# Order of work in the first and last channel pair of a chunk, in a fused state-space and FFN layer on one core

## What is computed

```python
# layer 1: state-space layer (DIN = 2048 channels, N = 16 states, R = 64, K = 4 taps)
h = layernorm(x)
xs, z = split(h @ in_proj_w)                 # 2048 channels each
xc = silu(conv_b + sum_k conv_w[:, k] * shifted(xs, k))
p = xc @ x_proj_w.T                          # 64 + 16 + 16 columns
dt_r, B, C = rmsnorm(p[:, :64]), rmsnorm(p[:, 64:80]), rmsnorm(p[:, 80:])
dt = softplus(dt_r @ dt_proj_w.T + dt_bias)
# per channel d and state n, over time t:
s[t, d, n] = exp(dt[t, d] * A[d, n]) * s[t-1, d, n] + dt[t, d] * B[t, n] * xc[t, d]
y[t, d] = sum_n s[t, d, n] * C[t, n]
x = x + ((y + D * xc) * silu(z)) @ out_proj_w.T
# layer 2: quantised FFN
x = x + layernorm(x) @ (scales * (codes - 128)).T + bias
```

## Time and profile before

| | |
|---|---|
| median of three runs | 4553.35 us |
| profiled execution | 4553.78 us, its span 4552.0 us |
| mean granted TensorE clock | 0.976 |
| TensorE (PE) busy | 4257.0 us, 94% |
| VectorE (DVE) busy | 4156.6 us, 91% |
| GpSimd (POOL) busy | 3887.0 us, 85% |
| ScalarE (ACT) busy | 3534.8 us, 78% |
| DMA | 828.91 MB, mean 182 GB/s |

### The profile page before, as it was taken

One profiled execution on the slowest core, in us unless ns is written; L12 is line 12 of the kernel. 1 busy time (PEld: TensorE's weight loads), 2 busy tenths in 40 slices (PEclk: granted clock), 3 DMA queues, 4 the chain that ended last, 5 costly groups with the idle time before them and its releaser, 6 DMA issues.

```text
span 4552.0 us, 77871 instructions
## 1 busy us (share of the span) xinstructions
PE 4257.0 (94%) x25632; PEld 3830.9 (84%) x25632; DVE 4156.6 (91%) x5745; ACT 3534.8 (78%) x8848; POOL 3887.0 (85%) x2894
## 2 busy tenths in 40 slices
PE   7688989999999999999999999999999999998879
PEld 6567778888888888888888888988888898897769
DVE  3899999999999999999999999999999999999871
ACT  3788787888888788787888888787888878888750
POOL 0898989989898998989899898998989899899870
PEclk9788999999999999999999999999999999998889
DMA  7545556575756657575575757557575665755452
GB/s 247 160 122 184 150 183 184 164 224 174 220 166 196 192 174 220 163 227 163 176 218 165 234 155 219 175 156 242 155 226 168 209 189 147 226 167 178 133 150 85
DMA packets 201348, 828.91 MB, mean 182 GB/s; under 512 B 25456, under 2 KB 34416, under 8 KB 151792
## 3 DMA queue, kind: packets, MB, share of 16 engines
q1 hardware_dynamic: 141296, 639.35, 38.6%
q0 software_dynamic: 41216, 151.01, 18.7%
q10 hardware_dynamic: 18432, 33.56, 2.0%
HBM read 634.57 MB, written 55.05 MB: 151 GB/s over the span
## 4 chain that ended last, share of the span: by engine, by line
PE 60%; POOL 19%; DVE 10%; issue 7%; ACT 2%; DMA 1%; SPq 0%; POOLq 0%; DVEq 0%; ACTq 0%
PE ys L646 14%; POOL dbx L494 12%; PE gx L626 12%; PE ys L606 12%; PE g L799 10%; PE g L721 7%; DVE hb L1416 6%; POOL half L518 3%; POOL half L512 3%; DVE gx L1298 1%; PE ys L636 1%; PE hb L901 1%; DVE hc L1364 1%; DMA ybuf<-in_wf_scales 1%; POOL hd L507 1%
## 5 line engine op out<-in xcount | busy, mean ns | idle before, releaser
L494 POOL TENSOR_TENSOR dbx<-dtx,bb 128x1024 f32<-128x1024 f32 x1024 | 2427.4, 2370 | 231.1 <-DVE hb L1416 183.8
L1416 DVE TENSOR_TENSOR_SCAN hb<-hb,dbx 128x512 f32<-128x512 f32 x2048 | 2495.6, 1219 | 55.4 <-ACT hb L1111 27.3
L1111 ACT ACTIVATE hb<-dt,a_neg 128x256 f32<-128x256 f32 x4096 | 1789.1, 468 | 66.3
L606 PE MATMUL ys<-half,ident 128*128 128x256 f32 x3072 | 811.6, 400 | 162.6 <-POOL half L512 93.6
L799 PEld LDWEIGHTS g<-wo,ybuf 128*128 128x128 f32 x7680 | 919.2, 194 | 30.7 <-issue 14.7
L646 PE MATMUL ys<-xnT,wz 128*128 128x256 f32 x4096 | 926.2, 385 | 11.4 <-DVE ybuf L1375 11.4
L799 PE MATMUL g<-wo,ybuf 128*128 128x128 f32 x7680 | 928.3, 277 | 8.4 <-issue 8.4
L626 PE MATMUL gx<-xnT,wx 128*128 128x256 f32 x3968 | 895.4, 383 | 21.5 <-issue 10.9
L646 PEld LDWEIGHTS ys<-xnT,wz 128*128 128x128 f32 x4096 | 782.6, 193 | 127.8 <-DVE ybuf L1375 22.8
L626 PEld LDWEIGHTS gx<-xnT,wx 128*128 128x128 f32 x3968 | 750.6, 192 | 127.3 <-issue 14.3
L606 PEld LDWEIGHTS ys<-half,ident 128*128 128x128 f32 x3072 | 567.4, 195 | 302.2 <-POOL half L512 125.0
(11 more groups left out here) (108 smaller groups left out, 3145.5 us busy)
## 6 DMA issues: line engine op xcount, KB each, us to landing
wz<-in_win SPq DMA_DIRECT2D x128, 1024.0 KB, 5.0
hd<-hd POOLq DMA_DIRECT2D x256, 512.0 KB, 6.3
wx<-in_win SPq DMA_DIRECT2D x124, 1024.0 KB, 5.0
wo<-in_wout SPq DMA_DIRECT2D x123, 1024.0 KB, 7.3
wf<-wf_scratch SPq DMA_DIRECT2D x113, 512.0 KB, 3.6
xc_scratch<-xcn ACTq DMA_DIRECT2D x128, 256.0 KB, 2.7
xcs<-xc_scratch SPq DMA_DIRECT2D x128, 256.0 KB, 5.2
bb<-bc_scratch SPq DMA_DIRECT2D x64, 512.0 KB, 9.6
```

The costliest lines, as they stand in the source:

```text
L494: nc.gpsimd.tensor_tensor(dbx[:, k % 2, :].rearrange("p (n t) -> p n t", n=NQ), dtx[:, S % 2, a, :].unsqueeze(1).to_broadcast([P, NQ, T]), ...
L606: mm = nc.tensor.matmul(ys[i // 3][:, 0:T], ident[:], half[:, n % PLACES, w * T:(w + 1) * T], start=False, stop=(i % 3 == 2 and w == 1), s ...
L1111: ins = nc.scalar.activation(h[:, m * T:(m + 1) * T], dt[:, j % 2, a, :], ACT.Exp, scale=a_neg[:, ds((2 * j + a) * N + 2 * v + m, 1)])
L1416: nc.vector.tensor_tensor_scan(h[:], h[:], dbx[:, k % 2, w * UW:(w + 1) * UW], 0.0, ALU.mult, ALU.add).then_inc(scans, 1)
```

## The change

In the last pair: TensorE's list gives x, dt and the three sums of tile 0 ahead of the last output part, which now stands directly ahead of z; the output part before is cut in two. ScalarE's x_taps and VectorE's taps move up, ahead of the softplus and of scan 13. In the first and last pair: VectorE's gate of tile 0 moves from behind product 11 to behind product 12, and the output add with the norm's statistics from behind product 12 to behind product 13. On SyncE the four loads of B's rows go ahead of the pair's weights, those of C in between and behind, and wx is loaded behind wo, dtw and C's third group. Ordinary pairs keep their order; `out_proj` only takes its bounds in another form.

```diff
@@ -384,11 +384,15 @@
                         sp.wait_ge(l2_tr, after(4 * (c - 1)))
                         sp.dma_start(xrow[:], x_rows[c + 2]).then_inc(xrow_in, 16)
                     if last and st.inproj:
+
                         bc_rows(c + 1)
-                        for q in range(2):
-                            load_b(c + 1, q)
-                            load_c(c + 1, q)
-                    if nx.x_job(nx_last):
+                        load_b(c + 1, 0)
+                        load_b(c + 1, 1)
+                        load_c(c + 1, 0)
+                        load_b(c + 1, 2)
+                        load_c(c + 1, 1)
+                        load_b(c + 1, 3)
+                    if not last and nx.x_job(nx_last):
                         load_pair(S + PAIRS + 2)
                     if nx.outproj:
                         sp.wait_ge(o_mm, after(S - PAIRS + 1))
@@ -397,9 +401,11 @@
                         sp.wait_ge(dt_mm, after(S + 2))
                         sp.dma_start(dtw[:], dtw_in[j_x]).then_inc(dtw_in_s, 16)
                     if last and st.inproj:
-                        for q in range(2, NQ):
-                            load_b(c + 1, q)
-                            load_c(c + 1, q)
+                        load_c(c + 1, 2)
+                    if last and nx.x_job(nx_last):
+                        load_pair(S + PAIRS + 2)
+                    if last and st.inproj:
+                        load_c(c + 1, 3)
                     if nx.next_scan(nx_last):
                         sp.wait_ge(z_mm, after(S + 2))
                         sp.dma_start(wz[:].rearrange("p a b -> p (a b)"), win[j_x + PAIRS]).then_inc(wz_in, 16)
@@ -781,10 +787,11 @@
                             pe.wait_ge(y_ready, after(2 * S + 1))
                         pair_z(S + 1, a)
 
-                    def out_proj(part):
+                    def out_proj(lo, hi):
+
                         if not st.outproj:
                             return
-                        if part == 0:
+                        if lo == 0:
                             pe.wait_ge(wo_in, landed(PAIRS // 2 + S - PAIRS + 1))
                             if first:
                                 pe.wait_ge(y_ready, after(2 * c * PAIRS))
@@ -792,7 +799,7 @@
                                 g1_after_f()
                             else:
                                 g1_after_o()
-                        for kt in range(part * TILES // 4, (part + 1) * TILES // 4):
+                        for kt in range(lo, hi):
                             for tt in range(TT):
 
 
@@ -801,7 +808,7 @@
                                                            (kt % 2) * T + tt * P:(kt % 2) * T + (tt + 1) * P],
                                                       wo[:, kt, :], start=(kt == 0 and tt == 0),
                                                       stop=(kt == TILES - 1), skip_group_check=True)
-                        if part == 3:
+                        if hi == TILES:
                             mm.then_inc(o_mm, 1)
 
                     def dt_proj():
@@ -822,27 +829,28 @@
                     if last and st.norm1:
                         norm1(0)
                         x_proj()
-                        out_proj(0)
+                        out_proj(0, 4)
                         norm1(1)
-                        out_proj(1)
+                        out_proj(4, 8)
                         norm1(2)
-                        out_proj(2)
+                        out_proj(8, 10)
                         norm1(3)
+                        out_proj(10, 12)
                         x_in_proj(0)
                         ss_transpose()
-                        out_proj(3)
+                        x_in_proj(1)
                         dt_proj()
-                        x_in_proj(1)
                         group(0)
                         group(1)
                         group(2)
+                        out_proj(12, 16)
                     elif first and st.ffn:
-                        out_proj(0)
-                        out_proj(1)
+                        out_proj(0, 4)
+                        out_proj(4, 8)
                         x_proj()
-                        out_proj(2)
+                        out_proj(8, 12)
                         norm2(0)
-                        out_proj(3)
+                        out_proj(12, 16)
                         norm2(1)
                         group(0)
                         dt_proj()
@@ -1232,14 +1240,14 @@
                     unit(11)
                     norm2(3)
                     unit(12)
-                    if not edge:
+                    if not edge or last:
                         x_taps()
                     dt_softplus()
                     unit(13)
                     first_decays_out()
                     second_skip_term()
                     unit(14)
-                    if edge:
+                    if edge and not last:
                         x_taps()
                     unit(15)
 
@@ -1509,16 +1517,23 @@
                     product(10)
                     scan(12)
                     product(11)
-                    y_gate(S, 0)
                     if not edge:
+                        y_gate(S, 0)
+                    if not edge or last:
                         taps()
                     scan(13)
                     product(12)
-                    add_out()
-                    norm_stats()
+                    if edge:
+                        y_gate(S, 0)
+                    else:
+                        add_out()
+                        norm_stats()
                     scan(14)
                     product(13)
                     if edge:
+                        add_out()
+                        norm_stats()
+                    if edge and not last:
                         taps()
                     scan(15)
                     product(14)
```

## The result

The changed kernel takes 4559.77 us (median of 22 runs, 4556.12 to 4564.15) against 4553.46 of the kernel before on the same chip (22 runs, 4549.43 to 4558.11): +6.3 us, a ratio of 1.0014 with a 95% interval of 1.0007 to 1.0020: slower, clear of noise, but by less than 0.2%. The busy times hardly moved (the page, part 1; before: the earlier trace rows); what moved is where engines wait.

What follows compares the result with a forecast made beforehand. VectorE and TensorE are both over 90% busy, no single bound; the loss sits at chunk edges. -11.4 - 2.7 + 0.5 + 3.7 + 21.6 + 0.7 = +12.4 us: 4566, own range 4556 to 4578, full range 4541 to 4585.

Steps and rivals of the forecast that it cites:

- its signs: Edges: z over 8 us at most, VectorE waiting 3 to 4 us at L1332, first pairs near 39 us.
- TensorE's and ScalarE's part: Last pair: sums done 2.5 us earlier, but taps ahead of the softplus; scan 13 waits 0.55 us.
- z late, at a steady clock zero: Edge: z starts at 2266.1 instead of 2264.01; VectorE's 1.95 us lead is all given back at L1332.
- B's rows: First pair: earlier B loads end GpSimd's dbx wait, 0.8 us per edge, bounds 0.5 and 0.84.
- First pair: Gate and output add move; the 1.62 us wait only shifts to scan 13; 0.15 us left, bounds 0 and 0.3.
- Chunk 15: Its first pair has no x projection to cover z, so gate and z come later: +3.7 us.
- Edges 0 to 1 and 1 to 2: Early edges: -2.7 us at 1 to 2, without FFN ahead; +0.5 and clock +0.7 at 0 to 1.
- The clock: TensorE's clock falls after 3.3 us idle ahead of z: 1.8 us per edge, 12 x 1.8 = +21.6, bounds 0.6 and 3.4.
- DMA: SyncE's reordered loads at the edge: as many bytes, each needed 10 us or more after its issue.
- Rival 1: The clock holds over TensorE's idle time, losing under 0.8 us per edge; B rows win: -9.9, 4543; chance 0.21.
- rival 3: Gate no longer waits, z's delay not felt, VectorE keeps 1.95 us per edge: 35 less, 4520; chance 0.04.
- Rival 2: Clock stays down through all of z: 3.4 us per edge instead of 1.8, +19 more, 4585; chance 0.13.

Runs made afterwards that it cites:

- The filler: Changed kernel plus six dummy matmuls between the last output part and z in each last pair; 4542.22 us, ratio 0.9982 to the kernel before.
- the early gate: Changed kernel with the last pair's gate of tile 0 back behind product 11, ahead of the filter; 4550.38 us, ratio 0.9999 to the kernel before.
- the best version: Changed kernel with last and first pairs' gate and first pair's output add at old places, xrow loaded in second pair; 4515.68 us, 0.9919 of the kernel before.

## Why the prediction was right, and where it was off

The direction and the path were as forecast: z late, an idle TensorE ahead of it, a fall of the clock, a wait at the output add. The size was half, 4559.8 against 4566, inside the forecast's own range. At +0.14% it also lies within the 0.2% of no change to which the prediction gave a chance of 0.16. Of its signs, z was over 8 us at 8 of 12 edges, the add waited 3.8 us at six and about 5 at two, and first pairs took 38.4 us on average (forecast near 39).

- **TensorE's and ScalarE's part** held to about a tenth: last pair 35.1 (forecast 35.2), wait at scan 13 0.47 (0.55), z 2.0 us later (2.1) behind 3.28 us idle (3.3), no wait at the gate.
- **z late, at a steady clock zero**: the add waited 2.11 us where the clock held (2.0), and such an edge is 72.21 us against the average of 73.13 before, -0.92 (forecast -0.95). The filler shows it at all twelve.
- **B's rows**: 0.72 us per edge by themselves (0.8 taken, bounds 0.5 to 0.84). What the prediction did not see is that late z would have covered most of their wait: in this kernel the new loads bring some 4 us, not 10. At full clock an edge takes 73.13 us with the old order and old loads (the average), 72.41 with the new loads alone, 72.4 with the new order alone and 72.21 with both. So either gain hides most of the other: the first to be made wins about 0.7 us, the second then 0.2. The sum, 0.8 for the loads and 0.15 for the rest, is not touched by it, since the edge with both came out as forecast.
- **First pair**: the wait only moved from the gate to scan 13, as said. Chunk 15: +4.1 us in the second pair, where +3.7 was forecast, and +0.5 in the first, which the sum had left out: scan 13 waits 2.47 us there instead of 1.83, behind the softplus.
- **Edges 0 to 1 and 1 to 2**: -2.1 up to chunk 2's last pair, against -2.7 + 0.5 + 0.7 = -1.5. This term is not resolved: in the twelve profiles that pair starts anywhere from 886.0 to 893.2 us, and at 891.1 and 889.2 in two of the changed kernel.
- **The clock**, 1.8 us per edge, was the term mis-sized. The granted clock held over z at 4 of 12 edges, fell for 3.4 us at 6 and for 6.8 us at 2: 72.2, 73.9 and about 75 us. (6 x 1.68 + 2 x 2.9) / 12 = 1.3 us per edge, so +15.9 instead of +21.6, which the filler's -15.7 confirms. The step that failed is the choice of one cost for every edge from two places: a fall mostly cost 1.7 us, near the 1.8 taken, but it did not come each time. That takes 5.7 us off the +12.4; most of the rest is that the profiled execution of the changed kernel is 2.4 us above its median.
- **Chunk 14**, +0.95 us, had no term. There one output part of the last pair took 3.2 us instead of 2.1, at an unchanged place, at a mean granted clock of 0.58 instead of 0.93: the clock came back later. It is not shown to be the change's doing: in the other runs the pair is 34.1 to 34.6, also with the old order (34.1 and 34.5).
- **DMA** cost nothing here, as said for the moved loads. The expectation of the early gate, 4521, took that over for an edge 2 us shorter, where the transfers of the first pair come too close together; that was wrong by 29 us.

Rival 1 (-9.9 us if the clock holds) describes the filler run, -8.8, to about 1 us; rival 3 (35 us less) needed z early, and the best version reaches 4516 by that way. Rival 2 was priced wrongly: it took 3.4 us for "all of z" at the lower clock. z takes 7.1 us at full clock, so all of it at 1.2 GHz would cost about 7 (an estimate, from twice the time); the longest falls seen at an edge, 6.8 us of low clock, cost 2.7 to 3.1.

The Trainium skill, "TensorE: Matmul & The Clock Gate", section "HAM oscillation", would have the clock hold over an idle time of this size. At 4 of the 12 edges the trace agrees, at 8 it does not: the same 3.28 us, between the same operations, was followed by a fall to 1.2 GHz.

## What to carry to other kernels

When an operation is put later to take a wait off one engine, look at which engine it releases, and what that one has left to do until then: here 2 us were won on VectorE and a TensorE idle time of 3.3 us was made, whose price is not the idle time but the clock behind it. Work that is wanted anyway should fill such a hole; where the order allows it, releasing early (the gate behind product 11, with x, dt and the sums ahead) wins twice. And before an edge is shortened, read the DMA share of its window and the landings in it: where the share is near 1, as 0.99 here, transfers that come closer together may land late, and a load that is not due moves first.

## What the runs showed of the hardware

- **The same idle time does not always cost the clock.** Behind 3.28 us idle at the same place, five executions of kernels with the late z (the changed kernel twice, and with the first pair, the loads or xrow's place put differently) kept 2.4 GHz over z at 17 of 60 edges, lost 1.7 us at 37 and some 2.9 at 6, in a different order of chunks each time. In the second pairs with the early gate, idle times of 2.2 to 3.3 us were followed by a fall in all five cases, those of 0.85 to 1.16 us in none of four. Two granted clocks of one kernel over z, held and fallen (columns as in the earlier trace rows):

```profile
920.98:928.15 7.17, 7.17 (x34) 6.34 (x35) 7.10 (x12) 4.29 (x15) 5.27 (x4) 1.00 1.04 350
1188.77:1197.60 8.83, 8.83 (x34) 7.50 (x35) 8.67 (x13) 5.87 (x20) 6.92 (x6) 0.81 1.04 362
```

- **In this pair DMA latency is a matter of what is asked for at once.** With the same transfers in a pair, and a DMA share of 0.99 or 0.94, a load of 1 MB took 4.9 us or 10.4 (over the chunks 4.9 to 7.9, or 7 to 13), and a 512 KB accumulation in SBUF 7.6 or 11.4 in the mean (the last of the pair up to 13, or up to 17), for issues that came some 2 us sooner behind the last pair's loads. The page's median over the whole kernel (hd: 6.3 us before, 5.8 with the early gate) shows nothing of it.
